# Value products of the first attention layer in one run per four steps instead of two

## What is computed

```python
B, L, S, D = 2, 512, 1024, 512          # x: (B, L, D), context: (B, S, D)
q = hidden_state @ Wq + bq              # 32 heads of 16, four to a key head
k = encoder_hidden_state @ Wk + bk      # 8 heads of 16
v = encoder_hidden_state @ Wv + bv
scores = jnp.einsum('bkgld,bksd->bkgls', q, k) * scale
scores = scores + encoder_attention_mask[:, :, None, :, :]
attn = jax.nn.softmax(scores, axis=-1)
out = jnp.einsum('bkgls,bksd->bkgld', attn, v)
out = out.transpose(0, 3, 1, 2, 4).reshape(b, l, H) @ Wo + bo
x = layer_norm(out + hidden_state) * gamma + beta
```

## Time and profile before

| | us |
|---|---|
| median of 3 runs | 2744.49 (2743.43 to 2745.05) |
| the profiled execution, its time | 2745.56 |
| its span, first to last instruction | 2743.8 |
| PE busy | 2632.0 (96%) |
| DVE, ACT, POOL busy | 1723.7, 1512.4, 1323.7 |
| mean granted clock of PE | 0.986 of full |

### The profile page before, as it was taken

How to read it: one execution, slowest core, us unless ns; L and a number is a source line. 1 busy time by engine, 2 the same in 40 slices (tenths; PEclk the granted TensorE clock), 3 DMA queues, 4 the chain that set the end, 5 groups by cost and what they waited for, 6 DMA issues and landing times.

```text
span 2743.8 us, 50326 instructions
## 1 busy us (share of the span) xinstructions
PE 2632.0 (96%) x17432; PEld 2148.6 (78%) x17432; DVE 1723.7 (63%) x2626; ACT 1512.4 (55%) x2360; POOL 1323.7 (48%) x750
## 2 busy tenths in 40 slices
PE   6899999999999999998978999999999999999989
PEld 5677778888887888886856777788888788888867
DVE  5799766565556565564157997756566566556541
ACT  4799654454545554544447995545554455554443
POOL 2333245566634666544423332456665446665643
PEclk8999999999999999999989999999999999999999
DMA  7311123544422535442463111244453234453512
GB/s 201 95 40 33 65 56 95 125 100 119 123 72 59 128 96 123 120 107 68 169 127 90 33 50 48 56 118 109 110 133 94 71 85 104 113 130 97 132 55 69
DMA packets 87731, 261.94 MB, mean 95 GB/s; under 512 B 19696, under 2 KB 33280, under 8 KB 81168
## 3 DMA queue, kind: packets, MB, share of 16 engines
q1 hardware_dynamic: 87568, 259.80, 36.2%
HBM read 135.45 MB, written 6.83 MB: 52 GB/s over the span
## 4 chain that ended last, share of the span: by engine, by line
issue 35%; POOL 29%; PE 29%; DVE 2%; DMA 2%; SPq 1%; ACT 1%; POOLq 1%; DVEq 0%; ACTq 0%
POOL pT L483 16%; PE ps_t L1081 5%; POOL wa L483 5%; PE ps_m L1096 4%; POOL v L483 4%; PE ps_m L958 4%; PE ps_s L1065 4%; PE ps_s L958 3%; PE ps_m L1081 3%; POOL wo L483 2%; PE ps_t L958 2%; PE ps_m L1134 1%; DMA scr_q<-parts 1%; SPq L361 1%; PE ps_m L1199 1%
## 5 line engine op out<-in xcount | busy, mean ns | idle before, releaser
L483 POOL TENSOR_TENSOR pT<-pT,pT 128x1024 fp32r<-128x1024 f32 x224 | 538.8, 2406 | 509.9 <-ACT pT L648 509.3
L648 ACT ACTIVATE pT<-pT 128x1024 fp32r<-128x1024 f32 x224 | 237.8, 1062 | 356.2 <-DMA pT<-pb 356.2
L774 ACT ACTIVATE p<-ps_s,nm 128x1024 f32<-128x1024 f32 x256 | 284.3, 1111 | 256.7 <-DVE nm L1577 255.9
L958 PE MATMUL ps_s<-kT,qT 128*128 128x512 f32 x1536 | 394.7, 396 | 11.3 <-ACT p L774 6.8
L1593 DVE STREAM_TRANSPOSE pb<-p 128x1024 f32<-128x1024 f32 x224 | 278.4, 1243 | 111.4 <-ACT p L774 101.3
L958 PEld LDWEIGHTS ps_s<-kT,qT 128*128 128x128 f32 x1536 | 279.3, 188 | 81.4 <-ACT p L774 20.1
L1574 DVE TENSOR_REDUCE nmx<-ps_s 128x1 f32<-128x1024 f32 x256 | 309.5, 1209 | 45.1 <-PE ps_s L958 45.0
L1504 DVE CUSTOM_DVE_ANT_0 sm<-ps_s,mask 128x1024 f32<-128x1024 f32 x256 | 309.6, 1210 | 9.7 <-PE ps_s L1065 8.5
L728 ACT ACTIVATE p<-sm,nm 128x1024 f32<-128x1024 f32 x256 | 293.9, 1148 | 36.5 <-DVE nm L1504 26.0
L958 PE MATMUL ps_t<-ctxT,wa 128*128 128x512 f32 x1080 | 262.2, 395 | 0.0
L958 PE MATMUL ps_m<-hT,wa 128*128 128x512 f32 x1008 | 247.6, 396 | 1.6 <-ACT g L932 1.6
(11 more groups left out here) (141 smaller groups left out, 4332.4 us busy)
## 6 DMA issues: line engine op xcount, KB each, us to landing
pT<-pb SPq DMA_DIRECT2D x896, 128.0 KB, 2.4
stg_qk<-in_wqk SPq DMA_DIRECT2D x40, 1024.0 KB, 7.4
stg_vo<-in_wo SPq DMA_DIRECT2D x48, 512.0 KB, 3.6
wob<-in_wo SPq DMA_DIRECT2D x32, 512.0 KB, 3.6
stg_vo<-in_wv SPq DMA_DIRECT2D x32, 512.0 KB, 3.6
q_stack<-scr_q SPq DMA_DIRECT2D x48, 128.0 KB, 4.4
st_ctx<-in_ctxT SPq DMA_DIRECT2D x8, 512.0 KB, 6.0
mask<-in_mask SPq DMA_DIRECT2D x2, 2048.0 KB, 13.1
```

What stands on the lines that cost most here:

```text
L483: return nc.gpsimd.tensor_tensor(out, x, f32(hi), ALU.subtract)
L648: return nc.scalar.activation(out, in_, ACT.Copy)
L774: nc.scalar.activation(p[t % 2][:], ps_s[t % 2][:], ACT.Exp, bias=nm[:, i:i + 1], scale=SCALE1, accum_out=sums[:, i:i + 1]).then_inc(exp_d ...
L958: mm = nc.tensor.matmul(out, lhs(x, c), rhs(y, c), start=start and c == 0 and i == 0, stop=stop and c == n_tiles - 1 and i == 2)
```

## The change

```diff
                     if t + 3 < STEPS0:
                         scores0(t + 3)
-                    if t >= GROUPS and t % 2 == 1:
-                        for i in (t % GROUPS - 1, t % GROUPS):
+                    if t >= GROUPS and t % GROUPS == 1:
+                        for i in range(4):
                             values0(t // GROUPS * GROUPS - GROUPS, i)
```

## The result

| us | before | after |
|---|---|---|
| median of 6 runs | 2743.96 (2739.94 to 2745.28) | 2770.06 (2764.66 to 2775.42) |
| the profiled execution, its time | 2745.56 | 2764.66 |
| its span | 2743.8 | 2762.8 |
| the stage of batch one, first maxima to last r | 262.33 | 273.76 |
| the stage of batch two | 262.32 | 273.30 |

The changed kernel is slower: ratio 1.0095, 95% interval 1.008 to 1.011. The medians differ by 26.1 us, and 26.4 were predicted. The profiled execution of the changed kernel is the lowest of its six; against the profiled one of before it is longer by 19.1 us.

The account below looks back on a forecast made before the run. PE was taken to set the pace, 15.23 us per unit. Per batch, stall 2.8, 13 units x 0.72 = 9.4 and end 1.0 gave 13.2, twice 26.4: 2770.9 us, range 2756 to 2787.

Parts of the forecast that it names:

- The seam: PE changing between full-width and 32-column work: about 0.28 us per half, 31 fewer per batch, 8.7 us of PE time.
- rival (1): First layer's attention: buffers cover the longer run, PE's time counts, fewer mode changes win; 2734 us, chance 0.06.
- The cycle: Four steps through the buffers take 7.84 us with the longer run; a unit becomes 15.95 us instead of 15.23.
- (h): On PE, from the start of a whole group's value products to the next transpose: 1.89 us.
- (e): From ACT's copy to the transpose into the bank it empties, second half of step t+4: 0.72 us.
- The turning point: Length of a value-product run on PE below which the change gains: about 1.5 us.
- The stall: PE's wait for r0 after each batch's first unit, moved from step 11 to step 9: 2.8 us per batch.
- nothing for steps up to 9: Start of the stage: the run at step 5, with two banks and ACT already waiting, was counted as costing nothing.
- The end: Last steps of the stage: step 125's run delays transposes by 0.88, 96 final loads become 64; taken 1.0 us.
- (2): First layer's attention: only the wait for r0 moves, the longer run costs what is saved; about 2751 us, chance 0.08.
- (3): First layer's attention: ACT needs 1.82 us per step, making a unit 16.35 us; 2781 us, chance 0.12.
- (4): TensorE's clock falls because it idles in every four-step cycle; far over 2800 us, chance 0.02.

Follow-up runs that it names:

- quarters: Each half of the value products cut in two, one block before an odd step's scores and one behind, against the kernel before: 2773.24 against 2747.09, ratio 1.0095.

## Why the prediction was right

**What bounds the kernel.** PE sets the pace before, 15.23 us per unit by the prediction and 15.216 by the average over 13 units. Changes on PE moved the time as PE's own cost (quarters: unit +0.97 for four seams).

**The seam.** Predicted 0.28 us, measured 0.24 by adding four. The Trainium skill (TensorEngine Tiling (Array Packing), Key Properties) says that a change of tiling mode drains TensorE; the runs here agree that such a change costs, with 0.24 us for a seam, though they don't show that the drain is all of it. What follows from that rule alone, fewer changes and so a faster kernel, did not come: rival (1) is out, since 31 seams less per batch came with a longer stage.

**The cycle.** This was the main step and it held: the burst is no longer covered, and PE waits for ACT. Link by link, predicted and then measured between 202.17 and 210.19 us: (a) 0.71, 0.70; (b) 0.60, 0.61; (c) 1.26, 1.26; (d) 1.14, 1.14, and the copy of rb 0.16, 0.16; (f) 0.50, 0.49; (g) 0.52, 0.53; (h) 1.89, 1.88 to the transpose of r, which takes 0.17 more. One link is off. (e), from ACT's copy to the transposed half that takes its bank, was 0.72 by the earlier trace rows and is 0.64: the copy starts at 208.53, the weight load of the second half at 209.17.

```profile
209.17 0.42 PEld L1081 LDWEIGHTS ps_t<-ident,p 128*128 128x128 f32 x4 [0.23 <-ACT pt L648]
```

The row used for the prediction, 63.85, was the matmul of a first half; its weight load starts at 63.82, 0.03 sooner. That leaves 0.05 between a first half and the second half that the link needs. The changed kernel shows 0.64 or 0.65 in each of 32 such waits. Why a first half takes longer isn't shown: it waits for the exponentials as well as for the copy, but those were over 0.5 us before the copy was. Twice 0.08 is 0.16, which is 15.95 less 15.78 up to rounding: the mis-sizing of the unit, 0.72 for 0.56 and so 2.1 us per batch, is this one link. It lies inside the bound that was set for it. PE's own need is 15.22 - 2 x 0.24 = 14.74 us per unit, so it stands idle for 1.04 us of each, where 1.3 were predicted.

**The turning point.** "About 1.5 us" is nearly right: runs of 1.45, 1.67 and 1.89 us gave units of 15.216, 15.256 and 15.78. With the 0.64 of link (e) the prediction's own sum gives 1.6, and the starts at 1.67 us say 1.64 to 1.69.

**The stall.** Predicted 2.8 per batch; from r0's transpose to step 20 the changed kernel takes 3.0 and 3.4 more, and with one burst alone the stages are 4.3 and 2.8 longer. That is agreement within the scatter of about 1 us, no closer. The reason given holds: work of two steps comes after the wait, and the wait ends when it did. Counted from the stage's first maxima r0's transpose stands at 39.02 and 38.51 us, before at 38.41 and 38.80; that it stands at 92.29 and not 93.5 is only because this stage began 1.9 us earlier. The pause itself was to grow to near 14 us and is 11.31 and 10.91. Two things went wrong there. The second half of the products now runs ahead of the pause, and its 0.88 us was not taken off the two steps of 1.90: 10.05 + 3.8 - 0.9 is 12.95, and the kernel with one burst alone has 13.00. And "nothing for steps up to 9" did not hold: behind the first burst, at step 5, PE waited twice and then ran for some 3.4 us at 1.2 GHz, as PE's rows and a stretch of the changed kernel show, with the same stretch of the kernel before as the last line:

```profile
67.80 1.95 PE L1096 MATMUL ps_m<-pt,v 128*32 128x128 f32 x64
...
72.79 0.66 PE L1081 MATMUL ps_t<-ident,p 128*128 128x128 f32 x4 [1.04 <-DVE pt L1512]
...
74.62 0.63 PE L1081 MATMUL ps_t<-ident,p 128*128 128x128 f32 x4 [0.74 <-DVE pt L1512]
```

```profile
75.00:78.50 3.50, 3.50 (x18) 2.91 (x17) 2.61 (x5) 2.59 (x6) 0.00 (x0) 0.53 1.04 168
```

```profile
75.00:78.50 3.50, 3.50 (x52) 2.79 (x46) 3.15 (x6) 3.07 (x6) 0.00 (x0) 1.00 0.82 138
```

In both batches the changed kernel needs 11.22 us from the first burst to the second. With r0 ahead of `value_rows` in every unit, the same two waits of 1.04 and 0.74 us (1.05 in batch two) follow the first burst, the clock stays at 1.00 in both batches, and it is 9.56 and 9.57 us, against 9.79 from the first half to the third with halves. So the burst at step 5 by itself lengthens nothing, and the half clock behind it takes 1.7 us, which the pause for r0 is shorter by: 13.00 - 1.7 is 11.3. These 1.7 us cost nothing only because the pause takes them up: cover, and not an absence of cost.

The start of the stage also scatters by itself. From the first maxima to those of step 8 the changed kernel needs 17.62 and 17.52 us, before 16.80 and 16.68, though the order of work up to there is the same: the clock came to 1.00 at 8.3 and 7.6 us behind the first maxima, and before at 5.4 and 5.0. The pause takes this up too. Behind the pause the clock was at 0.50 for 3.4 and 3.2 us here and for 4.6 and 3.7 before, so "the same in both" holds only to about 1 us.

**The end.** Predicted 1.0, measured 0.5. The stage of batch one ends at 327.04 us and not near 331: 1.9 of the difference is its earlier beginning, and the rest is what the sum was too high by.

**The sum.** Predicted 13.2 us per batch, measured in the stages 11.4 and 11.0: the cycle sized 2.1 too high in each, the end 0.5 too high, the stall 0.2 and 0.6 too low, and 0.6 and -0.3 us came ahead of r0's transpose, for which nothing was counted. Together 22.4 where 26.4 were predicted; the medians have 26.1. That the total agrees so closely is therefore partly luck. The profiled execution doesn't close the gap but widens it: the stages are 22.4 us longer, the first one begins 1.9 us earlier, the way from the last r of batch one to the next first maxima is 4.4 shorter (1103.4 to 1099.1) and the rest of batch two 2.9 longer (1060.5 to 1063.4), together 19.1. The stretches outside the stages, whose code is the same, scatter by that much between kernels: 1106.8 and 1063.2 with bursts from step 13 on. Whether the 4 us between the stages and the medians is such scatter or something that the change brings, no run here tells apart; it stays open.

**The rivals.** (2), only the stall moves, is out: bursts without the stall term cost 19.5 us. (3), ACT's pace as the limit with a unit of 16.35, is out: 15.78. (4) is out for the long stretch, where the clock stays at 1.00 though PE idles several times in every cycle; the clock fell behind the first burst only, for 3.4 us, where the pause hid it.

## What to carry to other kernels

A chain of engines that hand on tiles through a few buffers covers a run of other work only up to a length, and that length can be worked out beforehand: add the starts along the cycle through the buffers, put the run in, and compare with what the busiest engine needs. Merging pieces costs nothing up to there (here up to 1.45 us) and costs beyond it, even though the engine that does the work has less to do. And look at what stands in order behind a wait before moving the wait forward: the larger find here was beside the change, a 10 us stall at the start of each stage that went away by swapping two pieces of work on GpSimd, 26 us or 0.9% faster.

## What was not expected of the hardware

- A second half that waits for ACT's copy to free its bank starts 0.64 us after the start of that 0.59 us copy. For a first half it is 0.69 by its weight load and 0.72 by its matmul. What makes the difference is open.
- Idle times of PE of at most 0.7 us, several in every 8 us, left the granted clock at 1.00 in the whole long stretch. A single one of 1.14 us in the first unit of the kernel before left it there too. Two of 1.04 and 0.74 us behind the first burst were followed by 0.50 for 3.4 us in both batches of the changed kernel and in batch two with r0 first in the first unit. In batch one of that kernel, and in both batches with r0 ahead in every unit, the same two waits left it at 1.00. What decides that is open. After the stall of 10 us it was 0.50 for 4.5 us, and with the stall gone it was 1.00 there; the mean over the execution rose from 0.986 to 0.992.
- Beyond what the buffers cover the loss has no soft start. From 1.67 to 1.89 us each of a unit's two cycles grows by 0.22, and r0's transpose, which now follows the burst, adds 0.11: 0.55 us, measured 0.52 (15.256 to 15.78). Up to 1.45 us the unit stays at PE's own 15.216.
